# A graph-attention layer pair on one core: f2 spread by DMA, and the heads' attention computed turned over

## What is computed

```python
h  = relu(layernorm(x))
Wh = einsum('bnf,hfo->bhno', h, W)                  # 4 heads of 256
f1, f2 = Wh . a[:, :O], Wh . a[:, O:]               # one number per node and head
e  = leaky_relu(f1[..., :, None] + f2[..., None, :], 0.01)
p  = softmax(where(adj > 0, e, -1e9), axis=-1)      # 512 x 512 per head
g  = elu(p @ Wh)                                    # heads side by side: 512 x 1024
out = elu(the same attention once more, one head, W_out [1024, 256], on g)
y  = out + relu(out @ w1 + b1) @ w2 + b2
x  = x + layernorm(y) * gamma + beta
h  = relu(layernorm(x))
x  = x + deg * (h @ Wi.T + b) + adj @ (h @ Wj.T)
```

## Time and profile before

| | |
|---|---|
| three runs | 1540.99 us median (1539.92 to 1544.33) |
| the profiled execution's own time | 1542.53 us |
| its span, first to last instruction | 1540.7 us |
| busy: PE, PE weight loads | 93%, 87% |
| busy: DVE, ACT, POOL | 74%, 69%, 15% |
| mean granted TensorE clock | 0.974 of full |

### The profile page before, as it was taken

The page is one execution under the profiler, slowest core; times in us unless marked ns, Lnnn a source line. Parts: engine busy times, 40 slices in busy tenths (PEclk is TensorE's granted clock), DMA queues, the critical chain, the costliest instruction groups (busy, mean ns, idle before and its releaser), DMA issues.

```text
span 1540.7 us, 28639 instructions
## 1 busy us (share of the span) xinstructions
PE 1428.9 (93%) x10792; PEld 1333.2 (87%) x10792; DVE 1136.4 (74%) x2836; ACT 1066.9 (69%) x1700; POOL 236.3 (15%) x254
## 2 busy tenths in 40 slices
...
DMA packets 30056, 33.04 MB, mean 21 GB/s; under 512 B 1248, under 2 KB 28896, under 8 KB 29792
## 3 DMA queue, kind: packets, MB, share of 16 engines
...
...
## 4 chain that ended last, share of the span: by engine, by line
PE 81%; ACT 8%; DVE 7%; issue 3%; DMA 0%; POOL 0%; POOLq 0%; DVEq 0%; ACTq 0%
PE psA L736 52%; PE psR L789 8%; PE psT L890 4%; PE psT L814 4%; PE psA L848 4%; PE psA L859 4%; ACT ff L389 2%; ACT arg L420 1%; DVE hx_lo L577 1%; PE psT L780 1%; ACT prob_hi L426 1%; ACT hx_hi L441 1%; PE psT L768 1%; DVE arg L609 1%; PE psT L747 1%
## 5 line engine op out<-in xcount | busy, mean ns | idle before, releaser
L736 PE MATMUL psA<-whx_hi,prob_hi 128*128 128x258 f32 x1024 | 303.4, 296 | 14.2 <-DVE fcol L588 13.6
L736 PE MATMUL psA<-whx_hi,prob_lo 128*128 128x258 f32 x1024 | 291.0, 284 | 0.0
L736 PE MATMUL psA<-whx_lo,prob_hi 128*128 128x256 f32 x1024 | 289.9, 283 | 0.0
L577 DVE TENSOR_TENSOR prob_lo<-psR,prob_hi 128x1024 fp32r<-128x1024 f32 x160 | 195.2, 1220 | 55.5 <-ACT prob_hi L426 55.3
L356 POOL TENSOR_SCALAR elu_ex<-elu_in 128x512 f32<-128x512 f32 x160 | 103.4, 646 | 854.1 <-ACT elu_in L432 702.1
L609 DVE CUSTOM_DVE_ANT_0 arg<-psT,mask 128x512 f32<-128x512 f32 x320 | 208.0, 687 | 27.4 <-PE psT L780 24.4
L416 ACT ACTIVATE arg<-arg,fcol 128x512 f32<-128x512 f32 x320 | 212.5, 714 | 18.0 <-DVE gmax L609 18.0
L420 ACT ACTIVATE arg<-arg,nmax 128x512 f32<-128x512 f32 x320 | 212.0, 712 | 10.5 <-DVE nmax L620 10.5
L736 PEld LDWEIGHTS psA<-whx_hi,prob_hi 128*128 128x128 f32 x1024 | 195.8, 191 | 23.0 <-issue 17.8
L736 PEld LDWEIGHTS psA<-whx_hi,prob_lo 128*128 128x128 f32 x1024 | 194.9, 190 | 4.9 <-issue 3.6
L736 PEld LDWEIGHTS psA<-whx_lo,prob_hi 128*128 128x128 f32 x1024 | 195.6, 191 | 0.0
...
## 6 DMA issues: line engine op xcount, KB each, us to landing
xin<-in_x SPq DMA_DIRECT2D x16, 512.0 KB, 4.0
xb<-in_x SPq DMA_DIRECT2D x16, 512.0 KB, 3.9
out_x<-xb SPq DMA_DIRECT2D x16, 512.0 KB, 2.9
...
hcat<-in_L_gnn_W_heads SPq DMA_DIRECT2D x2, 512.0 KB, 8.1
...
xb<-in_L_gnn_W SPq DMA_DIRECT2D x1, 512.0 KB, 6.6
```

Of the source, the lines that this page charges most:

```text
L577: return dve.tensor_tensor(out=dst, in0=src, in1=hi.bitcast(fp32), op=ALU.subtract)
L736: i = pe.matmul(o, a, b_, start=(k == 0), stop=(k == n - 1))
```

## The change

- f2 goes to all partitions by two DMAs for each head: a column of 512 numbers out to a row of a DRAM scratch tensor, then that row to 128 partitions of `f2bc` in SBUF (two slots). `f2rows`, `spread` and their buffers go.
- In the heads' `attend` the operands change places: Wh is stationary, the probabilities move (256 columns), and the output has features on partitions. `turn2` goes: ACT and POOL write `hx` hi and lo straight from the unit's ELU. The output attention keeps its old form, without the columns of ones.
- The row sum comes from the Exp of `args` (`accum_out`); DVE takes its reciprocal (`rinv`), and POOL scales the probabilities in `arg` ahead of `turn_p` (`scale`).
- ELU reads the attention's result from PSUM: `elu_low` moves from POOL to DVE, and the pair of psA is free only after `elu_out`.
- b2 is added to `wk` by POOL (`add_b2`), in place of the four matmuls.
- The five tables are new. W_out, a_out, b_gc and b2 are loaded later, into other buffers.

The diff of the steps, cut:

```diff
+            def f2(c):
+                h = c.info
+                head = unit_number[c.b, h, 0] // 2
...
+                    sp.wait_ge(m1_read, 2 * H * c.b + 2 * h + 2)
+                    column = fcol[:, :, h, 1]
+                wait(sp, max_made, 4 * (head - F2S + 1))
+                sp.dma_start(f2_rows[head % 4].rearrange("(n q) -> q n", q=P), column, allow_slow_non_contiguous=True).then_inc(f2_out, 16)
+                sp.wait_ge(f2_out, 16 * (head + 1))
+                sp.dma_start(f2bc[:, head % F2S, :], f2_rows[head % 4].partition_broadcast(P)).then_inc(f2_spread[head % F2S], 16)
...
+            def scale(c):
+                pool.wait_ge(rinv_made, c.unit + 1)
+                for n in range(2):
+                    i = pool.tensor_scalar(arg[:, c.abuf, n, :], arg[:, c.abuf, n, :], rinv[:, c.abuf, n:n + 1], None, ALU.mult)
+                i.then_inc(p_scaled, 1)
+            def hx_lo_(c):
+                pool.wait_ge(hx_hi, head_unit(c.b, c.h, c.u) + 1)
+                pool.tensor_tensor(out=hx[1][:, 2 * c.h:2 * c.h + 2, c.u * HN:(c.u + 1) * HN], in0=elu[:, c.buf, :, :],
+                                   in1=hx[0][:, 2 * c.h:2 * c.h + 2, c.u * HN:(c.u + 1) * HN].bitcast(fp32), op=ALU.subtract).then_inc(hx_lo, 1)
+            def add_b2(c):
+                pool.wait_ge(o_turned, c.b + 1)
+                pool.tensor_tensor(out=wk[:, :, :], in0=wk[:, :, :], in1=b2_bc[:, None, :].to_broadcast([P, NC, F]),
+                                   op=ALU.add).then_inc(b2_added, 1)
...
-                    i = act.activation(a[:, n, :], a[:, n, :], ACT.Exp, bias=nmax[:, c.abuf, n:n + 1])
+                    i = act.activation(a[:, n, :], a[:, n, :], ACT.Exp, bias=nmax[:, c.abuf, n:n + 1], accum_out=rsum[:, c.abuf, n:n + 1])
...
+            def hx_(c):
+                act.wait_ge(elu_out, c.unit + 1)
+                wait(act, m2_done, NC * (c.b - 1) + 2 * c.u + 2)
+                act.activation(hx[0][:, 2 * c.h:2 * c.h + 2, c.u * HN:(c.u + 1) * HN], elu[:, c.buf, :, :], ACT.Copy).then_inc(hx_hi, 1)
...
             def rowmax(c):
-                dve.wait_ge(f2_spread, c.unit // 2 + 1)
+                dve.wait_ge(f2_spread[head % F2S], 16 * (head // F2S + 1))
...
-                    dve.tensor_tensor_reduce(out=arg[:, c.abuf, n, :], in0=psT[:, bank_of(c.h), :], in1=mask[:, 2 * c.u + n, :],
+                    dve.tensor_tensor_reduce(out=arg[:, c.abuf, n, :], in0=f2bc[:, head % F2S, :], in1=mask[:, 2 * c.u + n, :],
...
-                dve.reciprocal(rec[:, c.buf, :], psA[c.pair][:, :, F]).then_inc(elu_rec, 1)
-                dve.tensor_scalar(elu_in[:, c.buf, 1, :], psA[c.pair][:, 1, 0:F], rec[:, c.buf, 1:2], None, ALU.mult).then_inc(elu_xd, 1)
+                dve.tensor_scalar(elu[:, c.buf, :, :], psA[c.pair][:, :, 0:F], 0.0, -3.0e38, ALU.min, ALU.max).then_inc(elu_low, 1)
...
-                dve.scalar_tensor_tensor(out=dst, in0=elu_ex[:, c.buf, :, :], scalar=-1.0, in1=elu_in[:, c.buf, :, :],
+                dve.scalar_tensor_tensor(out=dst, in0=elu[:, c.buf, :, :], scalar=-1.0, in1=psA[c.pair][:, :, 0:F],
...
             def turn_p(c):
-                pe.wait_ge(arg_exp, c.unit + 1)
+                pe.wait_ge(p_scaled, c.unit + 1)
...
+                        terms = [(whx[:, j, c.h, part], whl[:, j, c.h, part], prob[0][:, c.buf, j, :], prob[1][:, c.buf, j, :]) for j in range(NC)]
+                    r = product(psA[c.pair][:, n, 0:F], terms)
                 r.then_inc(att_done, 1)
-                lend((c.pair,), (elu_xa, c.unit + 1), (elu_xd, c.unit + 1))
+                lend((c.pair,), (elu_out, c.unit + 1))
...
-                    pe.matmul(y, pick[:, 1, :], brow[:, :], start=True, stop=False)
```

More of the change, by code:

```diff
@@ L20 @@
+    ("m1", (1, 0), 1), ("turn_p", 7, 2), ("turn_out", 0, 3), ("attend", 6, 2),
 ]
 ACT_STEPS = [
[L22 to L24 removed]
[3 rows of a table removed]
[L28 removed]
@@ L29 @@
[L29 to L32, removed]
+    ("probs", 7, 3), ("turn_out", 0, 4), ("args", 9, 3), ("elu_exp", 6, 3), ("ffn1", 0, 4), ("m1", (1, 1), 2), ("hx", 6, 3),
@@ L37 @@
[L37 to L46, removed]
@@ L47 @@
-    ("elu_in", 9, 1), ("turn2", 1, 1), ("norm_ff_out", 0, 2), ("elu_out", 9, 1), ("turn_in", 0, 0), ("mix2", 0, 1),
-    ("turn2", 2, 1), ("m1", (0, 0), 0),
+    ("probs", 2, 3), ("m1", (3, 1), 3), ("rowmax", 5, 4), ("rinv", 4, 4), ("elu_low", 1, 3), ("rowmath", 5, 4),
+    ("probs", 3, 3), ("elu_out", 1, 3), ("elu_low", 2, 3), ("turn_gc", 0, 5), ("elu_out", 2, 3), ("rowmax", 6, 3),
+    ("elu_low", 3, 3), ("rinv", 5, 4), ("rowmath", 6, 3), ("elu_out", 3, 3), ("probs", 4, 4), ("conv_in", 0, 5),
@@ L49 @@
+    ("elu_out", 0, 2), ("m1", (3, 0), 2), ("rowmax", 4, 3), ("rowmath", 4, 3),
 ]
 POOL_STEPS = [
-    ("norm_gc", 0, 3), ("elu_low", 0, 1), ("elu_low", 1, 1), ("elu_low", 2, 1), ("elu_low", 3, 1), ("elu_low", 4, 2),
-    ("elu_low", 5, 2), ("elu_low", 6, 1), ("elu_low", 7, 1), ("norm_in", 0, 0), ("elu_low", 8, 1), ("x_beta", 0, 2),
-    ("norm_ff", 0, 2), ("elu_low", 9, 1), ("gamma", 0, 2),
+    ("scale", 8, 3), ("scale", 9, 3), ("add_b2", 0, 4), ("norm_in", 0, 1), ("hx_lo", 6, 3), ("scale", 0, 2), ("hx_lo", 7, 3),
@@ L74, in gnn_kernel @@
     ARGS = 3
+    F2S = 2
     x_v = x.rearrange("b (c p) f -> b p c f", p=P)
@@ L232, in gnn_kernel @@
         UNITS = [(0, 0), (0, 1), (1, 0), (1, 1), (BACK, 0), (BACK, 1), (2, 0), (2, 1), (3, 0), (3, 1)]
-        UNIT_STEPS = ("rowmax", "rowmath", "args", "turn_p", "probs", "attend", "elu_in", "elu_low", "elu_exp", "elu_out")
+        UNIT_STEPS = ("rowmax", "rowmath", "args", "rinv", "scale", "turn_p", "probs", "attend", "elu_low", "elu_exp",
+                      "elu_out", "hx", "hx_lo")
         IN_PSA = ("m1", "attend", "mix2", "ffn1", "ffn2", "conv_in")
```

275 lines of the change are left out of this document (114 added, 161 removed), and 7 rows, old and new, of tables (ACT_STEPS, PE_STEPS).

## The result

The changed kernel takes 1799.97 us (median of four runs, 1797.81 to 1811.14), the kernel before 1540.76 beside it: a ratio of 1.1692, 95% interval 1.164 to 1.1743. The forecast was 1457, so it is wrong in sign, and 343 us off. The profiled execution took 1797.8 us, the shortest of the four.

The account below looks back on a forecast made before the run. PE, busy 93% of the span, was taken as the bound. Removed work of 7.7 us a batch less a 2.2 us wait gave 88 us in all; 1542.5 - 88 + 4, less 1.5 for the median, gave 1457, range 1410 to 1508.

Parts of the forecast that it names:

- PE, removed: PE work dropped from each batch (turn2, f2rows, spread, b2 and a wait of m1): 7.7 us a batch.
- D: Time of f2's two DMAs together: 2.5 us for the column plus 3.2 for the broadcast, 5.7 us.
- Where D decides: Head 1: PE waits ahead of attend 8 if the two f2 DMAs together take over 3.5 us.
- the 2.2 us a batch of the forecast: PE's predicted wait ahead of attend 8, with f2's two DMAs taking 5.7 us together.
- The scale: Twenty POOL instructions a batch priced like elu_low at 0.65 us, 13 us; covered by three arg buffers.
- The rival of DVE and POOL: DVE and POOL exclude each other; ten rowmax pairs lose 0.65 us each, half reaching PE: 1509 us, chance 0.18.
- DVE keeps 18 us of air in a period: Argument against DVE and POOL delaying each other: DVE has 18 us idle in each period.
- The pair held too long: The pair of psA comes back to PE only behind elu_low, Exp and elu_out: slower, 1585 us, chance 0.08.
- The sum: Whole run: 7.7 - 2.2 = 5.5 us a batch saved, 88 in all, giving 1457 us.
- a landing is over 8 us: Sign named for the forecast being wrong: a DMA takes more than 8 us to land.
- PE's share under 90%: Sign named for the forecast being wrong: PE's busy share in the middle of the run falls under 90%.

Follow-up runs that it names:

- 16-byte version: The changed kernel with f2's column written as 128 pieces of 16 bytes in place of 512 of 4, computation complete: 1570.1 us, ratio 1.0179.

## Why the prediction was wrong

**PE, removed.** The steps are gone and the other rows hold, but for b2: "0.31, four times: 1.2". That was the distance from one matmul of b2 to the next piece of work; the chain shows it as 0.12 with 0.86 for the four behind it, and ffn2 without b2 is one row of 3.46 where four pairs took 3.92. So it is 0.46 a batch, and the sum about 7.0, not 7.7; 12 us of the run.

**D, the largest error.** "The first moves 2 KB in 512 pieces: I take 2.5, near the 2.9". It took 8.8. The number of pieces stood in the text, and so did a row of that kind, b1c with 256 pieces of 4 bytes in 7.7 us; it was set aside "as b1c had megabytes ahead of it". The row chosen as nearest had 512 KB in large pieces. The broadcast was put at 3.2 and took 4.8, or 3.7 in the 16-byte version. The fixed 2.0 us for a DMA in the Trainium skill (DMA: Bandwidth & Descriptors, section Anatomy of one DMA — SWDGE (gpsimd) path) gave an estimate of 4.6 for D, further off still: as it stands there it doesn't count the pieces. The trace's 2.0 us is for 128 pieces of 16 bytes, and the 8.8 for 512 of 4 isn't in it. The upper end, 15.4, held the measured 13.6, and was dropped from the range. D by itself doesn't give the sign: with D at 5.7 the kernel took 1570.1, still slower than before. The sign was lost in two steps together, this one and the terms put at nothing below, the exclusion and the scale's way to PE.

**Where D decides.** The forecast named head 1 and said heads 2, 3 and 0 had "ten us and more", and that on SP's queue "nothing is late". It read rowmax 1 as head 1's, but unit 1 is the second half of head 0; head 1's f2 is first asked for by rowmax 2, and isn't on the chain. Head 0 is, with its DMA behind the store that waits for `xb`, and so is BACK, named with room up to about D = 6. At D = 5.7, on the other hand, the 2.2 us a batch of the forecast don't appear: in the 16-byte version `rowmax` waits 12.5 us in all, under 1 a batch, and the whole kernel is 16 us, 1.0 a batch, above the one without DMAs.

**The clock** had no term. In the middle it was 0.91 to 0.93 in the mean for 1.00, and the same matmuls were busy 58 us longer than without the DMAs, of which an unknown part is time of the kernel.

**The scale.** "Twenty scale instructions of the same form and size" as elu_low, 0.65. The shape was the same, the operation was not: 1.63, so POOL has 54 us of work in a batch (861.6 / 16) and not 32. With no DMA in the way the difference costs 33 us. That scale "is covered because three arg buffers let rowmax run ahead of PE" failed too: PE waited 54.9 us for it in the changed kernel and 44.5 with no DMA.

**The rival of DVE and POOL** was right in mechanism and by the rule of the Trainium skill (SBUF — State Buffer, section SBUF: two separate sides), with which the earlier trace rows and the row at 863.81 both agree. Of its price, `rowmax` alone was counted. The rule speaks of an instruction with two SBUF inputs, and `zneg` is one, of the least size and on the path. Mending it alone is worth 41 us without the DMAs and 45 with them and the 16-byte column (1570.1 to 1525.2). "DVE keeps 18 us of air in a period" was no shelter: what counts is who waits behind the blocked instruction.

**The pair held too long** is no main cause: the run that gives it back early is level with the one that holds it, and PE's waits for `elu_out`, which it removes, were 20.1 us in all.

**The sum.** Of 343 us between forecast and result, 246 are the column's DMA. The other 97 stand against a sum that had 2.2 x 16 = 35 us of stall which the kernel without DMAs can't have; without that the forecast is 1422, and the gap 132. By edits made each on that kernel, 41 are zneg and 33 the scale's operation, and by the chain 12 are b2: 86. They were not run together, and the misses above show that such gains don't add, so the last 46 stay open; the further collisions of `rowmax` (920 to 950 ns, 20 times a batch), the fixed order, the 0.19 us for which ACT now reads out each row sum, where 0.1 was taken, and the mean granted clock, 0.953 with no DMA for 0.974 before, are where they can lie. What the profile was to show came out as "a landing is over 8 us" and PE's share under 90%, the two signs named for being wrong.
